# Softmax denominators summed on VectorE, with two 16-column products in place of products over ones

## The reference

```python
q, k, v = (einsum('ntc,hdc->nhtd', x_q, w) for w in (w_q, w_k, w_v))   # 16 heads of 64
a = einsum('nhtd,nhsd->nhts', q, k) / sqrt(64)
a = where(causal_forbidden, -inf, a)          # t = 1024
a = softmax(a, axis=3)
y = einsum('nhts,nhsd->nthd', a, v).reshape(4, 1024, 1024)
return y @ w_o
```

## Time and profile before

| | |
|---|---|
| median of 3 runs | 2227.13 us (2226.99 to 2232.01) |
| the profiled execution | 2232.77 us, its span 2231.0 us |
| PE busy | 2145.5 us, 96% |
| DVE busy | 1464.9 us, 66% |
| POOL busy | 1386.4 us, 62% |
| ACT busy | 1002.0 us, 45% |

### The profile page before, as it was taken

How to read it: one execution, slowest core, us unless ns; L and a number is a source line. 1 busy time by engine, 2 the same in 40 slices (tenths; PEclk the granted TensorE clock), 3 DMA queues, 4 the chain that set the end, 5 groups by cost and what they waited for, 6 DMA issues and landing times.

```text
span 2231.0 us, 34077 instructions
## 1 busy us (share of the span) xinstructions
PE 2145.5 (96%) x12130; PEld 1594.9 (71%) x12130; DVE 1464.9 (66%) x3340; ACT 1002.0 (45%) x1903; POOL 1386.4 (62%) x1250
## 2 busy tenths in 40 slices
PE   6998899999999999999999999999999899999997
PEld 4545788889876666766657666567666588899997
DVE  5365598676757667466774577874876646975553
ACT  4312453454445555345554355542554425434443
POOL 6313676677547776466674576664677846777774
PEclk8999999999999999999999999999999999999999
DMA  4533554565432212222322231221221244545552
GB/s 132 168 111 100 134 131 110 137 159 126 114 86 67 58 32 74 67 56 69 77 58 58 66 86 48 58 67 58 67 77 30 67 133 119 141 111 139 133 144 29
DMA packets 145048, 206.04 MB, mean 92 GB/s; under 512 B 19432, under 2 KB 112112, under 8 KB 144880
## 3 DMA queue, kind: packets, MB, share of 16 engines
q1 hardware_dynamic: 120304, 170.30, 25.6%
q0 software_dynamic: 24576, 33.57, 9.0%
HBM read 130.03 MB, written 39.85 MB: 76 GB/s over the span
## 4 chain that ended last, share of the span: by engine, by line
PE 73%; DVE 8%; POOL 4%; issue 3%; ACT 2%; DMA 1%; SPq 0%; another core or an unknown queue 0%; POOLq 0%; DVEq 0%; ACTq 0%
PE psum L1303 12%; PE psum L1324 11%; PE psum L1450 11%; PE psum L1352 7%; PE psum L1415 7%; PE psum L1431 6%; PE psum L1475 5%; PE psum L1366 4%; PE psum L1380 3%; PE psum L1460 3%; POOL t_acc L2408 2%; DVE f_hlo L2147 1%; DVE f_hhi L2145 1%; PE psum L1271 1%; PE psum L1393 1%
## 5 line engine op out<-in xcount | busy, mean ns | idle before, releaser
L1718 ACT ACTIVATE t_p<-psum 128x512 f32<-128x512 f32 (+3 forms) x768 | 323.8, 492 | 293.8 <-PE psum L1431 284.2
L2408 POOL TENSOR_TENSOR t_acc<-t_acc,t_p 128x1024 f32<-128x1024 f32 (+3 forms) x256 | 417.6, 1631 | 14.2 <-ACT t_p L1718 0.5
L2327 POOL TENSOR_TENSOR f_wlo<-f_wst,f_whi 128x256 fp32r<-128x256 f32 x256 | 222.1, 927 | 152.7 <-ACT f_whi L1651 152.7
L1324 PE MATMUL psum<-f_whi,f_hhi 128*128 128x256 f32 x1024 | 294.9, 288 | 6.6 <-DVE f_hlo L2147 6.6
L1450 PE MATMUL psum<-t_p,t_v 128*64 128x512 f32 (+3 forms) x1536 | 288.8, 496 | 7.4 <-POOL t_p L2388 7.4
L1324 PE MATMUL psum<-f_whi,f_hlo 128*128 128x256 f32 x1024 | 289.4, 283 | 0.0
L1324 PE MATMUL psum<-f_wlo,f_hhi 128*128 128x256 f32 x1024 | 289.2, 282 | 0.0
L2145 DVE CAST f_hhi<-f_h 128x512 fp32r<-128x512 f32 x256 | 142.0, 555 | 211.2 <-ACT f_h L1669 174.2
L1669 ACT ACTIVATE f_h<-psum 128x512 f32<-128x512 f32 x256 | 153.2, 599 | 278.5 <-PE psum L1303 250.0
L1415 PE MATMUL psum<-t_qa,t_ka 128*128 128x512 f32 (+3 forms) x768 | 222.1, 369 | 1.8 <-DVE t_mx L2193 0.7
L2408 POOL TENSOR_TENSOR t_acc<-t_p 128x768 f32<-128x768 f32 x64 | 134.6, 2104 | 135.2 <-PE psum L1460 131.9
(11 more groups left out here) (290 smaller groups left out, 4411.4 us busy)
## 6 DMA issues: line engine op xcount, KB each, us to landing
f_wst<-in_L_ffn_w SPq DMA_DIRECT2D x64, 1024.0 KB
t_ka<-t_ka SPq DMA_DIRECT2D x64, 256.0 KB, 3.2
t_qb<-t_qa SPq DMA_DIRECT2D x64, 256.0 KB, 3.9
t_wk<-wkT SPq DMA_DIRECT2D x32, 256.0 KB, 4.0
t_wq<-wqT SPq DMA_DIRECT2D x32, 256.0 KB, 4.0
t_wv<-wvT SPq DMA_DIRECT2D x16, 512.0 KB, 5.0
normal<-f_xy SPq DMA_DIRECT2D x5, 1024.0 KB, 10.3
a_x<-in_L_attn_a_x SPq DMA_DIRECT2D x4, 1024.0 KB, 7.8
```

The source lines that it names most:

```text
L1324: m = pe.matmul(out, h[:, js], w[:, f, :], start=(f == 0 and a == 0 and j % 2 == 0), stop=(f == FT - 1 and a == 2), skip_group_check=True)
L1718: act.activation(p[:, i, q0:], k.bank[bank][:, q0:], ACT.Exp, scale=1.0 / float(np.sqrt(k.DH))).then_inc(k.drained[bank], 1)
L2327: m = pool.tensor_tensor(t["wlo"][n % 2][:, i, ks], t["wst"][:, i, ks], t["whi"][n % 2][:, i, ks].bitcast(F32), ALU.subtract)
L2408: pool.tensor_tensor(acc[:, :, q0:], (p0 if kt == 1 else acc)[:, :, q0:], p[:, :, q0:], ALU.add).then_inc(k.p_acc, 1)
```

## The change

The two products over ones (512 columns each) go. In their place DVE transposes the whole accumulator (128 x 1024) in 32x32 blocks, and sums over runs of 32 columns, which leaves `part`: 128 x 32, four partial sums per query, one in each group of 32 partitions (`fold_sums`). PE adds these four with a constant matrix `fold` (128 x 64, ones where the row and the column agree modulo 32): two products of 16 columns. DVE takes the reciprocal straight from PSUM, without the transpose that was there.

`fold_sums` stands at the start of the step three pairs behind the chunk's end, ahead of that step's sums and scores; the products (`divide`) and the reciprocal (`sum_rows`) move one step later, into the step of the scaling. POOL's first sum of a new accumulator now waits for DVE's transpose in place of PE's product. The transposed accumulator (`turned`) takes the place of both `den` tiles, so `fold_sums` waits until POOL has read the `den` of the chunk before. `fold` itself is made at the start by two reductions.

```diff
-        self.d_den = Marks(s("dve_den"), "reciprocal", "rows")
+        self.d_den = Marks(s("dve_den"), "turned", "part", "rows")
...
-        t["den"] = [sb("t_den", [P, BANK]) for _ in range(2)]
+        t["turned"] = sb("t_turned", [P, 2 * BANK])
+        t["den"] = [t["turned"][:, c * BANK:(c + 1) * BANK] for c in range(2)]
+        t["part"] = sb("t_part", [P, 2 * BANK // 32])
...
+        def fold(n):
+
+            if ends(n - 3):
+                self.fold_sums(*pairs[n - 3][:2])
+
         def finish(n):
 
-            if ends(n - 3):
-                self.divide(*pairs[n - 3][:2])
+            if ends(n - 4):
+                self.divide(*pairs[n - 4][:2])
+                self.sum_rows(*pairs[n - 4][:2])
             if 0 < n <= len(pairs):
                 u, c, kt = pairs[n - 1]
                 self.weigh(u, c, kt)
                 self.weigh(u, c, kt + 1)
-            if ends(n - 3):
-                self.sum_rows(*pairs[n - 3][:2])
             if ends(n - 4):
                 scale(*pairs[n - 4][:2])
...
                 u, c, kt = pairs[n]
+                fold(n)
                 sums(n, 0)
...
     def divide(self, u, c):
+        n = BANK // 32
         bank = self.take(("den", u, c), self.work_bank())
-        self.wait_ge(k.p_acc, k.sum_count(u, c, k.KPC * (c + 1) - 1))
+        self.wait_ge(k.d_den.sem, k.d_den.at(2 * u + c, "part"))
         for i in range(2):
-            m = pe.matmul(k.bank[bank][i * DH:(i + 1) * DH, :], k.ones[:, 0:DH], t["acc"][(2 * u + c) % 2][:, i, :],
+            m = pe.matmul(k.bank[bank][i * DH:(i + 1) * DH, 0:n], k.fold[:], t["part"][:, i * n:(i + 1) * n],
                           start=True, stop=True, skip_group_check=True)
...
+        for n in range(0, k.DH, 32):
+            dve.tensor_reduce(k.fold[:, n:n + 32], k.ident[:].rearrange("p (g d) -> p d g", d=32), AX.X, ALU.add)
...
+    def fold_sums(self, u, c):
+
+        k, dve, t = self.k, self.e, self.k.t
+        chunk = 2 * u + c
+        self.wait_ge(k.p_acc, k.sum_count(u, c, k.KPC * (c + 1) - 1))
+        if chunk:
+            self.wait_ge(k.p_yt, chunk)
+            self.wait_filled(("den", (chunk - 1) // 2, (chunk - 1) % 2))
+        dve.transpose(t["turned"][:], t["acc"][c][:].rearrange("p i q -> p (i q)")).then_inc(k.d_den.sem, 1)
+        self.wait_ge(k.d_den.sem, k.d_den.at(chunk, "turned"))
+        dve.tensor_reduce(t["part"][:], t["turned"][:].rearrange("p (n j) -> p n j", j=32), AX.X,
+                          ALU.add).then_inc(k.d_den.sem, 1)
+
     def sum_rows(self, u, c):
-        den = t["den"][c]
-        if chunk > 1:
-            self.wait_ge(k.p_yt, chunk - 1)
-        dve.transpose(den[:], k.bank[bank]).then_inc(k.drained[bank], 1)
-        self.wait_drained(("den", u, c))
-        dve.reciprocal(t["rden"][chunk % 2][:, :], den[:].rearrange("p (n j) -> p n j", j=32)[:, :, 0]
-                       ).then_inc(k.d_den.sem, 1)
+        dve.reciprocal(t["rden"][chunk % 2][:, :], k.bank[bank][:, 0:BANK // 32]).then_inc(k.drained[bank], 1)
 
     def scale_rows(self, u, c):
-        self.wait_ge(k.d_den.sem, k.d_den.at(chunk, "reciprocal"))
-        dve.transpose(t["den"][c][:], spread(t["rden"][chunk % 2][:], 2, 32)).then_inc(k.d_den.sem, 1)
+        self.wait_drained(("den", u, c))
+        dve.transpose(t["den"][c], spread(t["rden"][chunk % 2][:], 2, 32)).then_inc(k.d_den.sem, 1)
...
         if kt == 1:
             if u:
-                self.wait_filled(("den", u - 1, c))
+                self.wait_ge(k.d_den.sem, k.d_den.at(2 * (u - 1) + c, "turned"))
```

More of the change, by code:

```diff
@@ L147, in constant_tiles @@
         self.minus_half = c("minus_half", [P, self.NBLK])
+        self.fold = c("fold", [P, self.DH])
         self.NCAND = 8
@@ L420 @@
     xt_block = qk_load = v_load = qk_product = qk_low = qk_double = v_product = skip
-    row_max = part_max = max_rows = high_scores = scores = weigh = add_up = divide = sum_rows = scale_rows = skip
+    row_max = part_max = max_rows = high_scores = scores = weigh = add_up = skip
+    fold_sums = divide = sum_rows = scale_rows = skip
     values_done = out_weights = out_load = out_product = out_add = skip
@@ L1006, in units @@
             for n in range(4):
+                fold(len(pairs) + n)
                 sums(len(pairs) + n, 0, 1)
@@ L2421, in scale_rows @@
         self.wait_ge(k.a_pvs, chunk + 1)
-        pool.tensor_tensor(t["yT"][c][:, hp, :], t["pvs"][chunk % 2][:], t["den"][c][:],
+        pool.tensor_tensor(t["yT"][c][:, hp, :], t["pvs"][chunk % 2][:], t["den"][c],
                            ALU.mult).then_inc(k.p_yt, 1)
```

## The result

The changed kernel takes 2244.84 us (median of 8 runs, 2238.45 to 2248.64), the kernel before 2227.22 us (8 runs, 2226.24 to 2232.42): a ratio of 1.0067 [1.0057, 1.0077]. The medians are 17.6 us apart; the ratio lies a little under their quotient of 1.0079 and stands for 14.9 us. It is slower, as forecast (2249 us). The profiled executions differ by less, 2243.9 against 2232.8 us, spans 2242.2 against 2231.0: before's took longer than all eight of its other runs, after's lies under its median. What the traces account for is therefore 11.2 us of the 17.6.

The account below looks back on a forecast made before the run. PE bounds the kernel, with DVE also nearly on the path from (3,0) to (6,1). Ordinary units +27.0, output units -4.0, last unit -1.3, constant +0.3 sum to +22 us: 2249 us, range 2218 to 2274.

Parts of the forecast that it names:

- What bounds: PE and DVE both nearly on the path from block (3,0) to (6,1), about 15 us; elsewhere PE alone.
- The fold, 2.52 us: DVE's added transpose 1.23 us and sum 1.21 us, plus handoffs of 0.03 and 0.05 us; ends 1.47 and 3.95.
- The small product, 0.35 us: PE's four added small instructions per chunk, both products of a unit on its path: +0.70 us a unit.
- The first fold: Chunk 1, ahead of block (0,0): 1.0 us gained in the ordinary unit read; mean shift at (4,0) -0.14 us.
- The second fold, +0.44 us: Chunk 0, ahead of block (5,1): DVE's path 5.86 us against 5.42 before, its lateness reaching PE in full.
- The unit: Ordinary unit: -0.14 + 0.44 + 0.70 = +1.00 us, times 27 = +27.0 us.
- the rival that the two sides cancel: DVE's added cost and PE's saving balance: 2222 to 2233 us, chance 0.18.
- the signs that it named: Profile after: attention's DVE busy up 110 us, PE idle 1.1 to 1.5 us, ordinary unit 1 us longer.
- The output units: Three units where DVE idles 5.11 and 3.44 us at the folds: (-2.02 + 0.70) x 3 = -4.0 us.
- The moved waits: POOL's first sum of chunk 1 starts 3 us sooner, worth 0; DVE's wait for `yT` has 2.2 us of cover.
- the third rival: POOL is late for the second fold's wait, holding DVE and the maxima behind it: 2282 us, chance 0.08.
- the fourth: PE stands for `part` at its product because DVE falls a whole step behind: 2266 us, chance 0.04.

Follow-up runs that it names:

- experiments 5 and 6: Changed kernel with the second fold moved behind block (7,1): 2232.23 us; with folds cut to 32 columns: 2191.70 us; with the fold's sum made twice: 2323.48 us.
- fill_both: Changed kernel with unneeded PE products filling its stands at (7,1) in each unit and at (4,0) in units without value projections: 2234.36 us, ratio 1.0022.
- late0: Changed kernel with only the second fold moved behind block (7,1), its product and reciprocal into the next unit's first step: 2232.23 us, ratio 1.0013.
- experiments 1 and 2: Changed kernel with unneeded products filling PE's stand at (7,1): 2238.67 us; also at (4,0) in units without value projections: 2234.36 us.
- ones_four_fill: Changed kernel with four chunks by products over ones again and block (7,1)'s second-head product issued five times: 2227.05 us, ratio 0.9985.
- fill_last: Changed kernel with the row maxima's scores of block (7,1), second head, issued five times: 2238.67 us, ratio 1.0035.
- before_delay: Kernel before with two unused sums on DVE ahead of block (0,0) in the four units without value projections: 2236.90 us, ratio 1.0033.

## Why the prediction was right, point by point

*What bounds.* Right. PE and DVE are both on the path between (3,0) and (6,1), and what is added to DVE there decides, shown by experiments 5 and 6. One piece of the evidence was misread: the score products of 0.67 us in the chain do not stand for a bank that DVE holds. The chain has the same 0.67 us at 1095.14, 3 us after DVE's last maximum of the unit (1092.12), and in the whole attention of the kernel before PE waits there hardly at all:
```profile
PE psum L1415 <- DVE t_mx L2193: 0.7, 2, 0.4
```
The idle times of DVE in the earlier trace rows carry the reading by themselves.

*The fold, 2.52 us.* The transpose took 1.24 us (1.23 forecast), the sum 1.22 (1.21); the next maximum begins 1.14 us after the sum does, so the fold holds DVE for 2.41 us (789.46 to 791.87). I had put the handoffs on top and overlooked that an instruction begins before the one ahead has ended. By the Trainium skill's rule ("VectorE: DVE Perf Modes", "The TRN2 errata"), each would take 1.13 us, an estimate; the trace has 1.24 and 1.22, as the rows of 512 columns had warned.

*The small product, 0.35 us.* The largest term that was mis-sized: 0.14 us (784.54 to 784.68 with the next product starting; 793.94 to 794.08). The eight products of 8 columns that I scaled from the earlier trace rows load weights of 128 columns each, 1.03 us from the first load to the end of the last, and start to start they took 0.89 us; the four of the fold load 64 columns each, in 0.20 us. For the narrower weights I had taken off 0.05 us; that they make the whole difference is not tested. Two of the small products a unit, 64 in all: 13 us of the sum were not there. The Trainium skill's table, in the same section, gives an estimate of 0.10 us, and the trace is nearer to it than to my row.

*The first fold.* Forecast: in an ordinary unit the full 1.0 us is gained. Measured from (3,0)'s last start to (4,0): 5.91 us before, 5.05 after, -0.86. In the units without value projections the fold was to be late by 1.46 us; `fill_both`, where the clock holds, has the first of them 1.6 us longer in all; the prediction's prices give 1.46 + 0.44 + 0.70 = 2.6, the measured ones 1.8. Right.

*The second fold, +0.44 us.* Measured +0.20 (5.41 to 5.61). The 0.24 between are the fold's 0.11 and block (5,1), 0.80 us instead of 0.94, since its maxima overlap too. That DVE's lateness reaches PE in full, the choice on which the forecast stood, is shown: PE stands 1.06 us in each unit (1.1 to 1.5 forecast), and moving that fold alone frees 1.06 us (experiment 5).

*The unit.* With the measured prices an ordinary one comes to -1.0 + 0.14 + 0.19 + 0.14 = -0.5 us; measured -0.86 + 0.12 + 0.20 + 0.17 = -0.37. The forecast had a mean of +1.00 over 27 units. The three sizes are worth -0.78 us a unit, 21 of the sum's 22 us. By its own steps the prediction, with right sizes, would have said "no change": the rival that the two sides cancel. Of the signs that it named, two failed by this: an ordinary unit is not 1 us longer but 0.4 shorter, and DVE's busy time in the attention rose by 90 us and not by 110.

*The output units*: -1.32 forecast, -1.5 measured. DVE's idle time ahead of them fell from 5.11 us to 2.77:
```profile
929.26 0.30 DVE L2206 CUSTOM_DVE_ANT_0 psum<-psum,t_mask 128x128 f32<-128x128 f32 x1 [2.77 <-PE psum L1403]
```

*The moved waits.* Worth nothing, as forecast, but not for the reason given. POOL's first sum of chunk 1 does not start 3 us sooner; it waits 3.17 us for ACT's exponentials where it had waited 3.55 for PE:
```profile
781.65 2.38 POOL L2428 TENSOR_TENSOR t_acc<-t_p 128x1024 f32<-128x1024 f32 x1 [3.17 <-ACT t_p L1729]
...
786.14 1.28 POOL L2442 TENSOR_TENSOR t_yT<-t_pvs,t_turned 128x512 f32<-128x512 f32 x1 [2.10 <-DVE t_turned L2246]
```
The product into `yT` ends at 787.42, 2.0 us ahead of the fold that waits for it: the third rival did not come. Nor did the fourth: PE has no wait at the small product (L1471) in the attention; it came only in `late0` (experiment 5).

*What was missing.* The clock: this is the step that failed, an omitted term and not a mis-sized one. I took PE's idle time as costing its length, and a PE that showed 1.00 over the attention as staying at 2.4 GHz. It goes to 1.2 GHz at eight places where the kernel before did not, up to 17.0 us in all; six of them, 13.6 us, lie behind stands that the prediction's steps make, and filling the stands gives 10 us back (experiments 1 and 2). So sign and size came out right by luck, because two misses ran against each other: prices too high by 21 us, a clock not thought of at up to 17. Stripped of the clock, the attention of the changed kernel is about as long as before's (13.4 - 17.0, -3.6 us or a little more), and `ones_four_fill` at 0.9985 says much the same from the other side.

Open stays why the clock falls behind one stand of 1.06 us and not behind some 25 others of the same length, and why falls that went at one place come at another (`fill_last`, `late0`). The 6.4 us between the profiled difference and that of the medians are not the clock's: 5.5 of them are before's profiled execution, longer than its median at a granted clock of 0.988, and 0.9 after's, under its median. Runs of the kernel before at the same granted clock of 0.987 have spans from 2224.6 to 2231.1 us; what makes these differ, no trace here shows.

## What to carry to other kernels

Work taken from the busiest engine and given to one with a third of its time idle pays only where that idle time lies: read the second engine's timeline around each place that it goes to, for every kind of unit and not for one. Of the 37 us that this change could give, its time on DVE took all and more; moving one of two folds and leaving four chunks alone turned +0.7% into -0.5%. Where a step makes a nearly always busy PE stand for a microsecond, price the clock with it, and look at the granted clock of the whole execution after each variant: a fall that is gone from one place may have come at another. And take an instruction's cost as the distance to the next one's start, not as its duration plus a handoff.

## What the runs showed of the hardware

The granted clock of PE fell to half behind stands of 1.06 to 1.87 us at six places of one execution, in a stage where PE is 95% busy; eight products then took 3.63 us instead of 1.94. Products of no use, issued into the stands of both folds, kept it at full in seven of the eight windows, and made the kernel faster by 10 us. A fall is not bound to its place: the same wait of about 2.2 us had one behind it in `before_delay` and none before, and in `late0` the falls came to 18.6 us at other places when the stand of 1.06 us was gone. Behind stands of 0.55 and 0.26 us in `before_delay` there was none.

Four products of 16 columns, with their weights of 64 columns, took 0.14 us to the start of what followed; eight of 8 columns with weights of 128 took 0.89. A transpose of 1024 fp32 columns from SBUF takes 1.24 us and a sum in groups of 32 takes 1.22, whose successor starts 0.08 us before it ends.
